# Graph message layer with residual layer norm: GpSimd waits for TensorE's progress ahead of every group of four indirect transfers

## The reference

```python
src, tgt = (x[row], x[col])
msg_input = jnp.concatenate([src, tgt, edge_attr], axis=-1)
h = jax.nn.relu(msg_input @ W1 + b1)
msg = h @ W2 + b2
attn_input = jnp.concatenate([msg, calibrated_vlm_conf], axis=-1)
attn_weight = jax.nn.sigmoid(attn_input @ Wa + ba)
gated_msg = msg * attn_weight
out = jax.ops.segment_sum(gated_msg, col, num_segments=x.shape[0])
...
x = _layernorm(x + out, axis=-1)
```

## Time and profile before

| | us |
|---|---|
| median of 3 runs | 845.35 |
| lowest and highest run | 837.32 and 855.74 |
| profiled execution, its own time | 835.85 |
| its span from first to last instruction | 834.1 |
| TensorE busy (matmul) | 458.1 |
| VectorE busy | 521.4 |
| ScalarE busy | 420.9 |
| GpSimd busy | 435.6 |
| 16 DMA engines, queue of SP / queue of GpSimd | 48.4% / 12.3% of the span |

### The profile page before, as it was taken

The page is one execution under the profiler, slowest core; times in us unless marked ns, Lnnn a source line. Parts: engine busy times, 40 slices in busy tenths (PEclk is TensorE's granted clock), DMA queues, the critical chain, the costliest instruction groups (busy, mean ns, idle before and its releaser), DMA issues. The chain is left out here.

```text
span 834.1 us, 9576 instructions
## 1 busy us (share of the span) xinstructions
PE 458.1 (55%) x2106; PEld 336.8 (40%) x2106; DVE 521.4 (63%) x2175; ACT 420.9 (50%) x1073; POOL 435.6 (52%) x449
## 2 busy tenths in 40 slices
PE   1466756365456665466664737364755638534281
PEld 0344544233335453355453625152634525332250
DVE  3697676797576866595857638395884544522162
ACT  0163765589264846372845707276483646411151
POOL 7362646465373657464514546627474365747410
PEclk9996969677777879676786758766787667857595
DMA  7679677599874956567568556457666544334101
GB/s 206 203 215 311 217 240 266 184 310 315 254 252 147 302 208 221 170 205 248 186 205 271 151 212 207 129 210 236 217 204 221 158 143 127 112 91 117 35 10 47
DMA packets 85504, 161.90 MB, mean 194 GB/s; under 512 B 13793, under 2 KB 51782, under 8 KB 85445
## 3 DMA queue, kind: packets, MB, share of 16 engines
q1 hardware_dynamic: 71493, 133.40, 48.4%
q0 software_dynamic: 13952, 27.87, 12.3%
HBM read 102.89 MB, written 59.16 MB: 194 GB/s over the span
## 5 line engine op out<-in xcount | busy, mean ns | idle before, releaser
L647 POOL DMA_INDIRECT rows_src<-x,src_list x120 | 118.2, 985 | 192.5 <-PE turn_ps L883 152.4
L925 PE MATMUL sum_ps<-gated,place 128*128 128x128 f32 x504 | 100.8, 372 | 169.7 <-DVE near L1318 87.6
L890 PE MATMUL hid_ps<-turned,w 128*128 128x512 f32 x294 | 175.1, 743 | 29.9 <-ACT turned L745 24.4
L763 ACT ACTIVATE nodes<-nodes,sc 128x128 f32<-128x128 f32 (+1 forms) x440 | 175.3, 485 | 0.0
L925 PEld LDWEIGHTS sum_ps<-gated,place 128*128 128x128 f32 x504 | 90.7, 273 | 190.6 <-issue 96.9
L745 ACT ACTIVATE turned<-turn_ps 128x512 f32<-128x512 f32 x147 | 79.4, 590 | 170.3 <-PE turn_ps L864 110.1
L1190 DVE BATCH_NORM_STATS2 stats<-nodes 128x6 f32<-128x128 f32 (+1 forms) x660 | 147.7, 279 | 22.2 <-DMA nodes<-x 12.5
L667 POOL DMA_INDIRECT out<-stash,row_idx x120 | 120.0, 1000 | 63.8 <-issue 36.0
L657 POOL DMA_INDIRECT stash<-x,dst_list x120 | 118.3, 986 | 36.6 <-issue 36.6
L900 PE MATMUL msg_ps<-w2x,hid 128*128 128x129 f32 x392 | 67.7, 326 | 109.5 <-ACT hid L750 56.4
L647 POOL DMA_INDIRECT rows_src<-x,src_near x76 | 77.2, 1016 | 84.0 <-PE turn_ps L883 59.1
(11 more groups left out here) (146 smaller groups left out, 527.2 us busy)
## 6 DMA issues: line engine op xcount, KB each, us to landing
nodes<-x SPq DMA_DIRECT2D x59, 704.0 KB
out<-nodes SPq DMA_DIRECT2D x59, 704.0 KB
attr_in<-edge_attr SPq DMA_DIRECT2D x49, 256.0 KB
near_dst<-line SPq DMA_DIRECT2D x19, 256.0 KB
near_x<-x SPq DMA_DIRECT2D x16, 256.0 KB
near_x<-x SPq DMA_DIRECT2D x20, 192.0 KB
out<-near SPq DMA_DIRECT2D x5, 704.0 KB, 6.6
near_x<-x SPq DMA_DIRECT2D x24, 128.0 KB
```

Of the source, the lines that this page charges most:

```text
L647: pool.indirect_dma_start(out=rows_src[:, k % RING, j, :], out_offset=None, in_=x[:, :], in_offset=bass.IndirectOffsetOnAxis(ap=idx[:, j:j ...
L763: return act.activation(row, row, ACT.Identity, scale=sc[0:parts, b % 2, 0, col:col + 1], bias=sc[0:parts, b % 2, 1, col:col + 1])
L890: last = pe.matmul(hid_ps[:], w1[:, c, :], turned[:, k % 2, c, :], start=(c == 0), stop=(c == 2))
L925: last = pe.matmul(sum_ps[:, use % 2, (w - low) * P:(w - low + 1) * P], place[:, b * P:(b + 1) * P], gated[:, k % 2, j, :], start=True, st ...
```

## The change

Two waits are added on GpSimd, both on the semaphore that TensorE raises after each part of a turn.

- Ahead of the target rows of step k: part 1 of turn(k - 1) must be finished.
- Ahead of each group of scatters of step k: for the first group part 2 of turn(k - 1), for the later ones part 3 of turn(k - 1).

`gather_dst` gets the step number as a second argument; for the first two groups, ahead of the loop, the awaited value is negative and `wait` leaves the wait out. Nothing else changes: number, order, size and contents of all transfers stay.

```diff
-            def gather_dst(i):
+            def gather_dst(i, k):
+
+                wait(pool, turned_ps_ready, 3 * (k - 1) + 1)
                 if i >= STASH_G:
...
-            gather_dst(0)
-            gather_dst(1)
+            gather_dst(0, 0)
+            gather_dst(1, 0)
             for k in range(2, K):
                 if k == 2:
                     pool.wait_ge(near_idx_ready, 1)
                 gather_src(k)
                 if is_list(k):
-                    gather_dst(STEPS[k][1])
-                for i in SCATTERS.get(k, ()):
+                    gather_dst(STEPS[k][1], k)
+                for n, i in enumerate(SCATTERS.get(k, ())):
+
+                    pool.wait_ge(turned_ps_ready, 3 * (k - 1) + min(n, 1) + 2)
```

## The result

| | kernel before | changed kernel |
|---|---|---|
| median, us | 843.28 (4 runs, 837.32 to 855.74) | 814.64 (4 runs, 814.2 to 818.36) |
| profiled execution, us | 835.85 | 814.85 |
| its span, us | 834.1 | 813.1 |

The ratio is 0.969 with a 95% interval of 0.963 to 0.976: the change is 3.1% faster. Predicted were 826 us for the median and 817 for the profiled execution.

What follows compares the result with a forecast made beforehand. GpSimd's long unbroken runs of transfers, which stop the other engines, were taken as the bound. 835.85 less 21 for four cuts plus 2 for late target rows gave 817 us profiled, scaled to a median of 826; range 795 to 860.

Steps and rivals of the forecast that it cites:

- The bound: Neither TensorE nor GpSimd bounds the kernel, but how GpSimd's 558 us of transfers are cut into unbroken runs.
- the waits at the new places: Sign: GpSimd waits at the groups of L657 and L667, where before it waited at L647 only.
- the run of 24: Sign: a run of about 24 GpSimd transfers after the part 1 of near turns.
- the cuts at steps 46 and 48: Sign: GpSimd's transfers are cut once at step 46 and once at step 48.
- 38 to 42 runs: Sign: GpSimd's transfers lie in this many unbroken runs instead of 36.
- nameless pieces of 15 us in the chain: Sign: pieces without an engine's name remain in the chain that ended last, only shorter in total.
- Most of what is cut here is joined there: Around step 39, held transfers join later ones into a run of 24, standstill 25.4 us against 25.5 before; nothing won.
- four cuts of 5.3 us: Over all 49 steps, the waits add four cuts to GpSimd's runs, winning 21 us.
- the standstill: Other engines nearly stop from 7.3 us into a GpSimd run until 2 us after it, about 367 us in all.
- The end: From turn 44 on: scatter 22 held, later scatters 26 to 28 beside free work; one cut more, 4.9 us won.
- Late target rows: Target rows of list steps after near steps, issued later, lose 0 to 62 us at some 13 places; 2 us taken.
- the rival: Target rows come late: TensorE waits up to 4.8 us at each of 13 places, 870 us; chance 15%.

Runs made afterwards that it cites:

- e7: Kernel before plus three clearings of a scratch tile behind every group of four transfers, standstill present: 726.61 us against 836.26, ratio 0.872.
- e9: Kernel before plus only the wait ahead of the target rows, standstill present: 830.62 us against 836.26, ratio 0.996.
- e8: Kernel before plus one clearing of a scratch tile behind every group of four transfers, standstill present: 817.14 us against 836.26, ratio 0.976.
- e2: Kernel before plus only the waits ahead of the scatters, no standstill: 690.02 us against 684.21, ratio 1.008.
- e11: Kernel before plus only the waits ahead of the scatters, another sitting, no standstill: 691.6 us against 681.2, ratio 1.016.
- e1: Kernel before plus only the wait ahead of the target rows, no standstill: 694.58 us against 684.21, ratio 1.014.
- e6: Changed kernel with its waits asking only for part 3 of turn(k - 2), so they never hold, against the kernel before, standstill present: 831.09 us against 834.7.
- e5: The changed kernel unaltered against the kernel before, no standstill: 698.33 us against 685.46, ratio of the medians 1.019.
- e10: Kernel before plus one clearing of a scratch tile behind every single transfer, no standstill: 714.31 us against 681.2, ratio 1.053.
- e12: Kernel before plus three clearings of a scratch tile behind every second group of transfers, no standstill: 691.99 us against 681.2, ratio 1.016.

## Why the prediction was right, and what in it was not

The direction and what bounds the kernel were right. The size was met partly by luck: the profiled execution was forecast at 817 us and took 814.85, because two errors in the sum cancel (below). The forecast for the median, 826 us against 814.64, is further off for one more reason. It was scaled up by the 1.1% by which the median of before lay above its profiled execution; in the changed kernel the two are equal.

**The bound: right, as far as the condition goes.** That other engines stop while GpSimd issues back to back, and that this and not the work of any engine sets the time, is shown by e7: no transfer and no computation less, 105 us of rest more, and 13% less time. What stops them no run shows. Of the signs for being right, the waits at the new places, the run of 24 and the cuts at steps 46 and 48 came; 38 to 42 runs (there are 46) and nameless pieces of 15 us in the chain (the longest is 10.52; the chain reaches back to 700 us only) did not.

**Where the new waits hold: the long holds right, the short ones missed.** Twelve holds of 4 to 22 us at target rows were forecast. The view of the waits also counts twelve, but only eight of them are longer than 4 us (5.2 to 17.3 us), and the timeline has 19 idle times over 0.6 us there. That the two twelves agree is chance. Of the cuts ahead of scatters all five that were forecast came, in steps 17, 22, 36, 46 and 48, and four that had not been forecast, in steps 33, 42, 45 and 47. Step 39 went as drawn: source rows alone, a hold, then a run of 24. The timeline of GpSimd, the starts of its runs in this stretch:

```profile
594.23 1.01 POOL L647 DMA_INDIRECT rows_src<-x,src_list  x1 [3.26 <-remote]
611.46 0.94 POOL L659 DMA_INDIRECT stash<-x,dst_list  x1 [12.44 <-PE turn_ps L868]
655.07 0.94 POOL L647 DMA_INDIRECT rows_src<-x,src_list  x1 [13.29 <-PE turn_ps L887]
```

From turn 37 to turn 40 the change loses there: 589.6 to 654.8, 65.2 us, against 56.3 before (609.4 to 665.7). "Most of what is cut here is joined there" was the right warning; that such a place costs was not in the sum.

**The number of cuts and their price: both wrong, and they cancel.** The sum had four cuts of 5.3 us, 21 us; there were ten, and 21 us came out, 2.1 us for each. The first miss is that short holds were not foreseen: 25 gaps of 1.2 to 4 us lie between the transfers of the changed kernel, 14 in the one before. Ahead of target rows and scatters, where the new waits are, there are 14 of them, and 1 before; a part of a turn comes there a little later than GpSimd has finished the group before. The prediction took those waits for satisfied. The second miss is the rule "all of the time from 7.3 us into a run to 2 us after it is lost, and a cut gives back 5.3". By it the change should have won 369 - 316 = 53 us. The rule also overstates the whole: it puts 367 us of the kernel before down to the standstill, but without the standstill the kernel is only 150 to 162 us faster (681 to 685 us against 835 to 843). e9, with the same sum of 314, shows that the rule doesn't carry over from one kernel to another, and e8 shows why it can't be complete: short gaps that break no run still gave 2.4%.

The traces show one thing that is wrong in the rule. On average the engines don't stop at 7.3 us into a run; they slow down from some 10 us on. Counted over all runs of a trace, by the time since the run began, this many instructions of TensorE (matmuls), VectorE and ScalarE start in 1 us:

| us into a run | before | full change | e9 | e8, short rests | e2, no standstill |
|---|---|---|---|---|---|
| 0 to 7.3 | 8.8 | 8.4 | 8.5 | 7.9 | 9.4 |
| 7.3 to 10 | 7.8 | 7.1 | 7.9 | 6.9 | 7.7 |
| 10 to 12.5 | 5.8 | 5.8 | 5.8 | 6.3 | 9.3 |
| 12.5 to 15 | 4.5 | 3.8 | 3.6 | 4.4 | 8.6 |
| over 15 | 1.7 | 2.6 | 1.4 | 3.5 | 7.2 |
| us spent over 15 us into a run | 136 | 80 | 100 | 117 | |

By the columns of before and e2 a run of 12 transfers, 15 us long, loses about 2 us, an estimate, where the rule takes 10 us for lost. The rule was fitted to two runs, of 31 and 35.6 us. So a cut would pay mostly where it shortens a run of over 15 us, and of these there are 18 before and still 15 after. The last row also puts the full change ahead of e9 and e9 ahead of the kernel before, which the count of runs does not; e8, at 818 us with 117, it doesn't explain, unless by the higher rate that its runs keep. This was counted afterwards in these five traces, and no run was made to test it.

I can't say what the right rule is. A rate that the chip keeps up with and a store that fills up would fit e8 (one transfer every 1.32 us on average in a run), e7 (every 1.51 us) and the short gaps alike, but no run tells it from the rule of unbroken runs.

**The end: right in its shape, too small in size.** Forecast was a cut ahead of scatter 22 and one ahead of scatter 26; both are there. But turn 45 came 13.5 us after turn 44, not 24.3, since scatter 20 was also held for a short time (a gap of 2.0 us at 706.5) and the run was 4 transfers shorter. Scatter 25 was held too, for 1.4 us, where a run of 24 had been forecast. From turn 44 to the end the change wins 119.7 - 108.4 = 11.3 us, forecast 4.9. Afterwards, as forecast, scatters 26 to 28 stand beside work that had been free: the time from turn 48 to the end grows by 8.9 us.

**Late target rows: small, as taken, with the standstill; without it the rival's sign is the true one.** 2 us were taken; TensorE waits there for 7.1 us in 3 places, 3.3 in 3 places before. Without the standstill it is 38.2 us in 16 places in the changed kernel, and 29.2 us in 11 places in e2, which holds no target rows. The three comparisons of a half of the change without the standstill give 1.008 to 1.016, and the medians of the whole change 1.019. That late rows make this loss is likely but not shown: the scatters' wait alone costs 0.8% and 1.6% (e2 and e11) and holds no target rows.

**Which half makes the gain: not settled.** The wait of the target rows alone is worth 0.4% and not the more than half that was expected of it in e1 and e9. That leaves the scatters' wait, alone or together with the other; the run that would tell them apart, e11, met no standstill.

## What to carry to other kernels

When engines wait for nothing that the profile can name, lay these times beside the timeline of GpSimd: if they start some microseconds into an unbroken row of its indirect transfers and end with it, try a rest of about a microsecond behind every few transfers (0.872 here) before anything cleverer. And measure such a change beside the old kernel in more than one sitting: the same rest cost 5.4% where the stall was absent, and the change of this case, 3.1% faster in one condition, was in the other about 1.9% slower by its medians, and each of its halves 0.8 to 1.6% slower. The rest of one clearing behind each group was the mildest: 0.976 with the standstill, 1.004 without.

## What the runs showed of the hardware that was not expected

- The kernel before takes 681 to 685 us or 835 to 843 us, the same program, in one case on the same chip. With the standstill SP's four loads took 14.12 us to issue and VectorE did nothing for 17 us beside a run of transfers; without it, beside a run of 104 transfers, the four loads took 3.74 us and VectorE was busy for 13.27 of 17 us.
- The traces differ in one more thing. Those with the standstill hold 5318 to 5558 records of semaphore updates (before, changed, e6, e8, e9), e7 in the same condition 7247, and those of e1 to e5 and e10 to e12 without it 14041 to 14509, of nearly the same programs. Most of what is missing are records of landed transfers (3630 before, 11726 in e2). So more than half of these records are missing with the standstill, and in e7 too, where the rests have ended the standstill, half are: the loss goes with the condition and not with the standing still itself. The Trainium skill, NOTIFIC — the notification-queue block, section 7.1, says that a full queue of such records can, in one of its modes, stall the engine that writes them; in that mode it loses none, and records are lost in others. The missing records agree with a path of records that is not emptied fast enough; no run here shows that this path is what stops the engines. Every timed run here has its span and granted clock recorded, so whether the standstill exists when nothing is recorded is open too.
- A GpSimd transfer of 128 rows costs 1.26 to 1.28 us from start to start (medians of the traces) in both conditions, rests aside; the standstill spares GpSimd and hits the others.
